# An audio tower in one kernel: zeros and slot arithmetic spread out, two pairs of heads per product in one unit, and a reordered end

## The reference

```
h   = sign-convolution(x), 3 taps -> (4, 748, 64), batch-norm scale and shift
qkv = layernorm(h) @ Wqkv + bqkv                     # 8 heads of width 64
score = q @ k / 8 per head;  attn = softmax(score)   # only the diagonal of attn is used:
av  = diagonal(attn) * v;  h = h + (av @ W0 + b0)
y   = layernorm(h)
# a binary tree of 255 nodes, 8 levels: each token walks down by the sign of y . w1[node]
out = h + sum over 8 levels of gelu(|logit|) * (y @ w2[node] + b2[node])
```

## Time and profile before

| | us |
|---|---|
| median of 3 runs | 474.11 |
| lowest, highest | 471.88, 476.61 |
| time of the profiled execution | 474.62 |
| its span, first to last instruction | 472.7 |
| chain of work that ended last: VectorE, issue, ScalarE, TensorE, GpSimd | 33%, 17%, 15%, 15%, 12% |
| busy: TensorE, VectorE, ScalarE, GpSimd | 352.7, 342.5, 324.0, 284.2 |

### The profile page before, as it was taken

The page is one execution under the profiler, slowest core; times in us unless marked ns, Lnnn a source line. Parts: engine busy times, 40 slices in busy tenths (PEclk is TensorE's granted clock), DMA queues, the critical chain, the costliest instruction groups (busy, mean ns, idle before and its releaser), DMA issues.

```text
span 472.7 us, 8346 instructions
## 1 busy us (share of the span) xinstructions
PE 352.7 (75%) x2606; PEld 248.5 (53%) x2606; DVE 342.5 (72%) x577; ACT 324.0 (69%) x832; POOL 284.2 (60%) x398
## 2 busy tenths in 40 slices
PE   1156896878789889777898769883512999999970
PEld 1144565655456555445664446552312777788860
DVE  0475969899788878998888998978530789955440
ACT  1363996788888998577898656758200799987760
POOL 4315748786867875584689662661552365666663
PEclk9996999989999999989999999995555999999995
DMA  4425243417998972131243130018915012120000
GB/s 95 128 62 136 53 113 81 101 39 172 178 187 160 151 182 47 53 97 29 71 113 97 38 82 1 3 42 116 118 31 139 23 36 56 33 54 6 12 15 5
DMA packets 58953, 37.27 MB, mean 79 GB/s; under 512 B 31661, under 2 KB 57607, under 8 KB 58906
## 3 DMA queue, kind: packets, MB, share of 16 engines
q1 hardware_dynamic: 54778, 33.81, 35.7%
q0 software_dynamic: 3328, 2.36, 2.0%
q10 hardware_dynamic: 800, 0.49, 0.5%
HBM read 11.42 MB, written 7.50 MB: 40 GB/s over the span
## 4 chain that ended last, share of the span: by engine, by line
DVE 33%; issue 17%; ACT 15%; PE 15%; POOL 12%; DMA 5%; SPq 1%; POOLq 0%; DVEq 0%; ACTq 0%
DVE nm L1392 14%; ACT Z L1192 10%; POOL out L726 8%; PE Z L923 6%; POOL pre L723 3%; DMA pre<-in_x 3%; DVE va L1421 2%; ACT q L1134 2%; DVE pre L1488 2%; ACT k L1134 1%; PE Z L843 1%; DMA pool_a<-pool_a 1%; DVE pre L1503 1%; DVE va L1437 1%; DVE pre L1665 1%
## 5 line engine op out<-in xcount | busy, mean ns | idle before, releaser
L1192 ACT ACTIVATE Z<-Z,nm 125x748 f32<-125x748 f32 x192 | 166.3, 872 | 61.5 <-DVE nm L1392 60.2
L1392 DVE TENSOR_REDUCE nm<-Z 125x1 f32<-125x748 f32 x192 | 175.4, 933 | 36.4 <-PE Z L923 30.0
L923 PE MATMUL Z<-pool_a 128*125 128x512 f16 (+1 forms) x768 | 162.0, 338 | 28.1 <-ACT Z L1192 23.4
L923 PEld LDWEIGHTS Z<-pool_a 128*125 128x125 f16 x768 | 87.7, 140 | 71.8 <-ACT Z L1192 46.0
L726 POOL DMA_INDIRECT out<-pre,va x44 | 44.7, 1017 | 35.1 <-POOL pre L723 35.1
L1665 DVE TENSOR_REDUCE pre<-va 128x64 f32<-128x512 f32 x44 | 45.7, 1039 | 5.8 <-ACT va L1275 2.4
L790 PE MATMUL Z<-xhT,wq 128*128 128x249 f16 (+1 forms) x192 | 32.9, 291 | 11.9 <-DVEq L1402 10.5
L1192 ACT ACTIVATION_READ_ACCUMULATOR Z<-Z,nm 125x1 f32 x192 | 41.2, 215 | 0.0
L652 POOL DMA_INDIRECT sorted_rows<-xrow,slot x24 | 30.4, 1266 | 15.3 <-DVE slot L1544 8.7
L620 POOL TENSOR_TENSOR va<-va 125x256 f32<-125x256 f32 (+2 forms) x54 | 29.6, 548 | 10.3 <-DVE va L1421 7.2
L596 POOL TENSOR_TENSOR pool_a<-q,pool_a 128x748 f16<-128x748 f32 x15 | 24.7, 1644 | 10.2 <-DVE pool_a L1349 9.1
(11 more groups left out here) (243 smaller groups left out, 667.1 us busy)
## 6 DMA issues: line engine op xcount, KB each, us to landing
pool_a<-pool_a SPq DMA_DIRECT2D x64, 187.0 KB, 3.3
pool_a<-pool_a SPq DMA_DIRECT2D x64, 93.5 KB, 2.2
sorted_rows<-zrow SPq DMA_DIRECT2D x1, 3640.0 KB, 23.8
va<-sorted_rows SPq DMA_DIRECT2D x12, 260.0 KB, 3.0
w<-in_L_ffn_w2s SPq DMA_DIRECT2D x1, 2048.0 KB, 16.5
pre<-in_x SPq DMA_DIRECT2D x4, 375.0 KB
pool_a<-in_L_ffn_w2s SPq DMA_DIRECT2D x1, 1024.0 KB
out<-pre,va POOLq DMA_INDIRECT x44, 2.2
```

What stands on the lines that cost most here:

```text
L923: last = mm(z[0:XP, c0:c1], kst[:, u % 3, a, hd, KST[t]:KST[t] + XP], qst[:, u % 3, hd, c0:c1], start=(a == 0), stop=(a == 1))
L1192: sc_.activation(z, z, ACT.Exp, bias=nm[0:XP, u % 4, i:i + 1], accum_out=sm[0:XP, u % 4, i:i + 1]).then_inc(s_exp, 1)
L1392: v.tensor_reduce(nm[0:XP, u % 4, i:i + 1], Z[n % 3][0:XP, 0:N], X, ALU.max, negate=True).then_inc(s_max, 1)
```

## The change

- **Zeros.** The memset of the leaf table is cut in five (64 x 1664), one in each of units 5 to 9, behind `qk_lo` on GpSimd. The table's column (`leaf_columns`) moves from unit 4 to unit 10, its bias row's DMA from behind the loads of unit 7 to behind those of unit 13.
- **Slot arithmetic.** The running sum is done in two halves of 375, in steps 1 and 3; the counts move from step 3 to 5. The f16 product is halved too and goes with its column instructions and `pf` to the next unit (10, 14): columns at step 1, halves at 3 and 5, `pf` at 7, `sl` from 9 to 10.
- **Unit 14.** In place of four products with one pair of heads each (`yp`, steps 4, 6, 8, 10) there are three with two pairs and two tiles each (`yq`, steps 7, 9, 11). GpSimd adds them in one go (`add_two`, three instructions) behind `ln2_squares`, in place of two `add_pair`.
- **End of the attention.** The last diagonal goes straight behind the last scores into `Z[0]` and waits for the exponentials instead of for a half of E. VectorE and ScalarE take it at step 0 of unit 16. The last pair's v products go from steps 5 and 6 to 1 and 2. VectorE does the last layer norm before the counts and ranks of sequence 2, whose `sl` moves behind the logits of sequence 3. The zeros of the low table start at step 0.
- **Output.** `own_slots(B - 1)` goes ahead of `low_columns`. GpSimd adds h for tile k + 1 before it scatters tile k; for overflow tiles VectorE adds h.

```diff
-            if 1 <= u <= NU and i < 3:
+            if 1 <= u < NU and i < 3:
                 f.append(("d", u - 1, i))
...
             if u == NU - 2:
-                f += {4: [("yp", LASTB, 0)], 6: [("yp", LASTB, 1)], 8: [("yp", LASTB + 1, 0)],
-                      10: [("yp", LASTB + 1, 1)]}.get(i, [])
+                f += {7: [("yq", 0)], 9: [("yq", 1)], 11: [("yq", 2)]}.get(i, [])
...
-                f += {(0, 8): [("A", b - 1, 0)], (0, 10): [("A", b - 1, 1)], (1, 10): [("pf", b - 1)],
-                      (2, 9): [("sl", b - 1)]}.get((ph, i), [])
+                f += {(0, 8): [("A", b - 1, 0)], (0, 10): [("A", b - 1, 1)], (2, 7): [("pf", b - 1)],
+                      (2, 10): [("sl", b - 1)]}.get((ph, i), [])
             if b == B - 1:
-                f += {(0, 0): [("A", b - 1, 1)], (0, 5): [("yp", NU - 1, 0)], (0, 6): [("yp", NU - 1, 1)],
-                      (0, 8): [("pf", b - 1)], (0, 10): [("sl", b - 1)], (1, 0): [("t", b, 0)], (1, 1): [("t", b, 1)],
-                      (1, 2): [("L", b, 0)], (1, 3): [("L", b, 1)], (1, 5): [("A", b, 0)], (1, 6): [("A", b, 1)],
+                f += {(0, 0): [("A", b - 1, 1)], (0, 1): [("yp", NU - 1, 0)], (0, 2): [("yp", NU - 1, 1)],
+                      (0, 8): [("pf", b - 1)], (1, 0): [("t", b, 0)], (1, 1): [("t", b, 1)], (1, 2): [("L", b, 0)],
+                      (1, 3): [("L", b, 1)], (1, 4): [("sl", b - 1)], (1, 5): [("A", b, 0)], (1, 6): [("A", b, 1)],
                       (2, 0): [("pf", b)], (2, 2): [("sl", b)]}.get((ph, i), [])
...
-                link(gp.memset(w7[D:P, :], 0.0))
-                pool.sem_inc(s_z7, 1)
+            def leaf_zeros(n):
+                c = LEAVES * E1 // ZPARTS
+                gp.memset(w7[D:P, n * c:(n + 1) * c], 0.0).then_inc(s_z7, 1)
+                pool.wait_ge(s_z7, n + 1)
...
+            def add_two():
+                pool.wait_ge(s_wyv, NT * (B - 1) + 3)
+                pool.wait_ge(s_hb, B)
+                hv = xrow[0:XP, TT - NT:TT, C_H:C_ID]
+                pw = two_prod[0:XP]
+                link(gp.tensor_tensor(pw[:, :, 0:P], pw[:, :, 0:P], pw[:, :, P:2 * P], ALU.add))
+                link(gp.tensor_tensor(hv, hv, pw[:, :, 0:D], ALU.add))
+                gp.tensor_tensor(hv, hv, pw[:, :, D:P], ALU.add).then_inc(s_hy, 1)
+                pool.wait_ge(s_hy, NT * (B - 1) + 1)
...
-                if u == NU - 2:
-                    add_pair(LASTB)
                 if 0 <= b < B - 1 and ph == 2:
                     ln2_squares(b)
                 if b >= 1 and ph == 3 and b < B - 1:
                     own_slots(b - 1)
-                if NU - 2 <= u < NU:
+                if u == NU - 2:
+                    add_two()
+                if u == NU - 1:
                     add_pair(u - 1)
...
             own_slots(B - 2)
+            own_slots(B - 1)
             pool.wait_ge(s_zl, LOWZ)
             low_columns()
-            own_slots(B - 1)
...
+            residual(0)
             for k in range(ST_TILES):
+                if k + 1 < ST_TILES:
+                    residual(k + 1)
                 rows_out(k)
...
                 if n == 0:
-                    take(("d", w))
+                    if w < NU - 1:
+                        take(("d", w))
+                    else:
+                        pe.wait_ge(s_exp, 2 * NT * NU - 2)
                     pe.wait_ge(s_prod, w + 1)
-                z = zone(("d", w))
+                z = zone(("d", w)) if w < NU - 1 else Z[0]
...
+            def two_pairs_out(n):
+                z = take(("yq", n))
+                for t in range(2 * n, 2 * n + 2):
+                    r0, g = v_tile(B - 1, t)
+                    zt = z[0:XP, t % 2 * 2 * P:(t % 2 + 1) * 2 * P]
+                    for a in range(2):
+                        mm(zt, xhT[:, r0:r0 + XP], mw[:, a, g * H * D:g * H * D + 2 * P], start=(a == 0), stop=False)
+                    last = mm(zt, pick[:, g, 0:XP], cb[:, 0:2 * P], start=False, stop=True)
+                last.then_inc(s_full, 1)
...
-                    if 1 <= b < B - 1 and (ph, i) == (1, 1):
-                        leaf_ranks(b - 1)
-                    if 1 <= b < B - 1 and (ph, i) == (1, 3):
-                        leaf_counts(b - 1)
-                    if 1 <= b < B - 1 and (ph, i) == (1, 5):
-                        rank_of_token(b - 1)
...
+                    if 1 <= b < B - 1:
+                        if (ph, i) == (1, 1):
+                            leaf_ranks(b - 1)
+                        if (ph, i) == (1, 3):
+                            scan(1)
+                        if (ph, i) == (1, 5):
+                            leaf_counts(b - 1)
+                        if (ph, i) == (2, 1):
+                            old_terms()
+                        if (ph, i) in ((2, 3), (2, 5)):
+                            rank_of_token(b - 1, (i - 3) // 2)
...
                     if u == NU and i == 8:
                         last_heads(NU - 1)
                         ln2_sums(B - 1)
                         ln2_last()
-                        rank_of_token(B - 2)
-                    if u == NU and i == 9:
+                        leaf_counts(B - 2)
+                        old_terms()
                         ln2_last_x()
+                        for n in range(2):
+                            rank_of_token(B - 2, n)
...
+            def add_residual(k):
+                dve.wait_ge(s_sl, k + 1)
+                o = yo[:, k % NO, :]
+                v.tensor_tensor(o, o, xs[:, (k // 4) % NX, k % 4, C_H:C_ID], ALU.add).then_inc(s_yov, 1)
```

108 lines of the change are left out of this document (76 added, 32 removed).

## The result

| | before | after |
|---|---|---|
| median of the runs, us | 474.75 (471.88 to 476.61, 4 runs) | 489.05 (486.67 to 490.24, 4 runs) |
| ratio to before | 1 | 1.03, 95% interval 1.023 to 1.037 |
| profiled execution, us | 474.62 (span 472.7) | 489.11 (span 487.4) |
| granted clock over the span | 0.911 | 0.894 |

Forecast: 466.3, faster.

What follows compares the result with a forecast made beforehand. VectorE was taken to bound units 9 and 13, three tied engines ordinary units, GpSimd's backlog the end. Terms -2.7 + 1.0 - 0.5 - 3.2 + 3.6 - 2.2 - 4.0 = -8.0 from 474.62 gave 466.6, predicted 466.3; range 461.5 to 471.

Steps and rivals of the forecast that it cites:

- Unit 2: Attention unit 2: without the 7.03 us memset, VectorE's held TENSOR_SCALAR and slow matmuls behind the pause go, -2.7 us.
- Unit 7: A zeros piece in unit 6 delays GpSimd's `ln2_squares`; VectorE waits, with unit 7's maxima behind that wait, +1.0 us.
- After the last scores: End of attention: earlier last diagonal and reordered work bring the last slots sooner, 32.0 us after the last maximum, -2.2 us.
- Output: Output stage: GpSimd's backlog goes during overflow tiles, so the end follows VectorE's last sum, -4.0 us.
- `low_columns`, behind the last scatters now, is covered by their landing and the load.: End of attention: moving `low_columns` behind the last scatters was to cost nothing.
- `group_slots` at step 8 falls beside GpSimd's two products of 1.6 and 1.76 us, 2.0 to 3.3: Unit 10: the moved `group_slots` costs VectorE 2.0 to 3.3 us beside GpSimd's products.
- unit 10 at +3.6: Unit 10: slot arithmetic moved in adds 3.3 to 5.5 us of work, about 1 hidden, so +3.6 us.
- the moved work costs its bare price: Unit 14: GpSimd is nearly idle, so the moved slot arithmetic costs only 3.3 us.
- Units 9 and 13: Slot arithmetic moved out shortens units 9 and 13, where VectorE is the bound, by 4.1 and 3.8 us.
- rival 2: Units 9, 10, 13, 14: moving slot arithmetic gives nothing, -3.7 becomes 0, total 470.0 us; chance 0.15.
- rival 3: Units 10, 14 and the end: GpSimd holds moved column instructions, eight holds of 1.3 us give 476.7 us; chance 0.05.
- Unit 15, +3.6: Unit 15: `add_two` ahead of `ln2_rstd` makes TensorE wait 2.6 to 3.1 us before transposes; with slower clock, +3.6 us.

Runs made afterwards that it cites:

- c_best1: Kernel after with `low_columns` first, slot arithmetic and output as before, unit 6's zeros behind `ln2_squares`, `add_two` behind `ln2_x`: 0.8% faster than the kernel before.
- b_overflow_residual: Kernel before with VectorE adding the residual of the overflow tiles, GpSimd still adding static ones right ahead of their scatters: 481.27 us.
- b_output_paced: Kernel before with the whole output change and a 128x640 memset behind each static scatter: static stage 52.1 us, no total time given.
- b_overflow_paced: Kernel before with VectorE adding the overflow tiles' residuals and a 128x640 memset behind each overflow scatter: 479.75 us.
- b_output_only: Kernel before with only the output change: static stage 53.8 us, no total time given.
- a_loads_first: Kernel after with TensorE's 16 leaf loads ahead of its waits for `low_columns`, tables and zeros: 14 us lower, ratio 0.997 to the kernel before.
- a_slots_back: Kernel after with the slot arithmetic of units 9, 10, 13 and 14 at its old places: unit 9 22.8 us, unit 10 16.1, no total time given.
- b_static_ahead: Kernel before with only the static residuals added one tile ahead on GpSimd: static stage 51.4 us, fastest execution 472.69 us.

## Why the prediction was wrong

**Right, with its mechanism.** Unit 2 (-2.7 said, -2.3 measured). Unit 7 (+1.0, +1.1), and c_best1 shows the cause by taking it away. "After the last scores" (-2.2, -1.9): 32.3 us from the last maximum to the last slots where 32.0 was said (the row has 338.77 where the prediction counts from 338.67). "Output", as the lag behind the last sum (-4.0, -4.1); that the backlog "is gone long before the last one, even if the pause of 0.79 stayed in all 32" is half borne out: in b_overflow_residual GpSimd catches up four tiles before the end, but its one long tile gave it 7.2 us of that, and in b_output_paced, without one, 26 us of backlog are gone only at the last tile. With a pause in the overflow tiles too (b_overflow_paced) 22 us are not made up.

**Failed steps, by size.**
1. *-4.0 as the whole term of the output.* VectorE's add is hidden, as said (overflow tiles -0.6). But a faster GpSimd scatters every 1.45 us in the static tiles. The prediction asked what stood behind its last scatter and not what its new cadence meets: +11.9 us, of which the output change alone carries 7.3 (b_output_only), the rest being first tiles at half clock (up to 383.9, 13 us behind the first transposes, where it is 3 to 6 in all other kernels) and more gaps. Shown: the output change makes it, its scatters carry it, its additions don't. Open: what makes TensorE's products late, and why a_loads_first escapes.
2. *"`low_columns`, behind the last scatters now, is covered by their landing and the load."* Its 1.1 us are covered. Who waits for it was not followed: TensorE, with 16 register loads of 0.65 us queued behind that wait, 10.6 us against a cover of some 4. +6.7, shown from three sides.
3. *"`group_slots` at step 8 falls beside GpSimd's two products of 1.6 and 1.76 us, 2.0 to 3.3", with unit 10 at +3.6, and in unit 14 "the moved work costs its bare price".* In unit 10 the step went from 1.23 to 4.91. In unit 14 GpSimd has no product then and the chain does take its bare 2.0, but in one step with a maximum and a weighing: 3.71, with a TensorE wait of 1.05. Unit 10 rose by 5.6, and the clock fell behind TensorE's wait of 2.52 there; unit 14 rose by 2.3, which isn't clear of the spread above. Units 9 and 13 gave 3.0 and 3.2 where 4.1 and 3.8 were said. Units 9 to 11 and 13 to 14 came to +2.1 where -3.7 was said; rival 2 (moving gives nothing) was nearer, and rival 3 had the mechanism (one element a partition held for 1.71 us instead of 0.15), with two holds in unit 10 (1.6 and 0.4 us) where it counted eight of 1.3 in all.
4. *Unit 15, +3.6.* It measured +3.1, but for another reason in this kernel: the steps 0 to 2 ran at 1.2 GHz (2.0 us each instead of 0.86, 1.30, 0.84), and that delay hid all but 1 us of the wait. The clock fell at 298.6, behind two TensorE waits of 1.05 and 1.27 us; all four kernels with this attention code have the three slow steps, none of the eight with the old one has. a_slots_back shows the wait alone: +3.25. That the term came within 0.5 us is luck.

The range held only independent errors of listed terms. Both large losses are in stages that had no term, so no width would have followed from them.

## What to carry to other kernels

When a call is moved past others in a queue, follow not only who is queued behind it but everything that stands behind each wait for it, register loads included: they are in no busy time. When an engine is made faster, ask what its transfers now meet, and try that edit alone. An arithmetic chain moved into a "free" slot takes the price of the neighbour's product there, and the clock may take the same again.

## What the runs showed of the hardware

- TensorE's `value_load` takes 0.65 us (load 0.30, register operation 0.15, check 0.02 and gaps), 16 in a row 10.6 us.
- TensorE's granted clock fell behind short waits of TensorE: 2.52 us in unit 10 (clock 0.86), 2.41 in unit 15 of a_slots_back, and 1.05 with 1.27 ahead of unit 15 (0.50 from 298.6 to 305.4).
- A VectorE addition with two SBUF inputs of one element a partition took 1.71 us beside GpSimd's product of 128x748 f32 (0.15 alone); a 128x96 one with three inputs 0.74 (0.35). Copies and a tensor_scalar just before, beside GpSimd's previous product, took 0.15 and 0.16. The Trainium skill, "GPSIMD Engine Reference", section "8. Key points", names contention for two SBUF inputs; here the trace agrees, unlike in the earlier trace rows, where GpSimd's instruction was a memset, which has no input.
- Scatters of GpSimd 1.45 to 1.65 us apart, with TensorE, ScalarE and VectorE in a tight loop: ScalarE's waits for TensorE's products add up to 9.3 us in 32 tiles at full clock (b_output_only) instead of 2.3, single ones up to 2.6 (b_static_ahead). At 2.1 us and more apart this was small or absent (2.3 and less); at 1.5 (a_loads_first) and 1.28 apart (overflow tiles of b_output_paced) absent too.
- A wait for a small memset on GpSimd's own queue costs more than the memset: 128x640 brought a tile from 1.28 to 2.41 us, 128x64 to 1.94.
